# Graph convolution kernel: products of one-hot tiles and of sheet blocks in alternating order, and a third buffer for one-hot rows

## The chip, the cores and the metric

The kernel runs on one core of one Trainium2 chip. The metric is the device time of the whole program in microseconds (us), the median of several runs. A core has five engines with a queue each: TensorE (PE, whose weight loads are shown apart as PEld), VectorE (DVE), ScalarE (ACT), GpSimd (POOL) and SyncE (SP). They meet only at semaphores.

## The reference, cut to what matters

Two graph convolutions with normalisations between them, and then a mixture of eight feed-forward experts over the same 12500 nodes. The change touches the sum over edges, which each of the two convolutions has once:

```python
def _hconv(x, src, dst, ew, w1, b1, w2, b2, g, b):
    h = jax.nn.relu(x @ w1 + b1)
    msg = ew[:, None] * h[src]                                   # 200000 edges, 256 channels
    agg = jax.ops.segment_sum(msg, dst, num_segments=x.shape[0]) # edges are sorted by dst
    h = agg @ w2 + b2
    return jax.nn.relu(_bn(h, g, b))
```

The edges are sorted by dst, and dst is 12500 times the square of a uniform number: the low nodes have very many edges, the high ones few.

## The kernel before

The function `aggregate(layer)` runs once for each convolution. It sums the edges in two ways.

**Groups of gathers.** Edges are cut into tiles of 128, and four tiles (GT) make a group. For every tile, GpSimd issues one indirect DMA that fetches 128 rows of h from DRAM into one of R = 24 buffers `G` (`gather`, L982; the trace names the buffers wst, f_xr, f_u and more). VectorE makes a 128x128 one-hot matrix for each tile (`onehots`, L1180, 12 buffers `OH`). TensorE multiplies them, eight matmuls of 128x128 for a group (L1065, which the trace shows as 16 passes, since an fp32 matmul has two). VectorE adds the result into `agg` at the group's window (L1276). Before gathering the first tile of a group, GpSimd waits until TensorE has done the group that last used those buffers, six groups earlier (`g_mm`). Layer 0 has 291 such groups (1163 gathers), layer 1 has 271 (1083 gathers).

**Low groups.** Edges of the lowest nodes aren't gathered. They fall into "hot" tiles of 128 edges, 400 in layer 0 and 80 in layer 1. VectorE makes one-hot rows of the sources (`hot_rows`, L1189, into one of two buffers `HW`), ScalarE makes one-hot columns of the destinations (`lows`, L1113 and L1117, `LO`), TensorE multiplies them into `pX` (`hot_products`, L1019, two matmuls for a tile, four passes, two buffers), and VectorE adds the product to a count matrix `A` (`hot_add`, L1207). Such matrices are stored to DRAM as "sheets" by SP and loaded again in batches, and TensorE multiplies sheet blocks with rows of h (`unit`, L1033, two matmuls for a block, four passes, into `pF`). When a sheet is complete, VectorE adds it to `agg` (`seg_add`, L1223).

The two kinds of work are woven by a table that the program works out when it is built: `hot_behind(layer, q)` and `units_behind(layer, q)` list the hot tiles and the blocks that stand behind group q. In layer 0 there are one to three hot tiles behind each of the groups 0 to 193 (343 columns for a matmul shortly before group 80, 147 to 245 from there on), and none to three blocks behind the groups from 39 to 282. In layer 1 two hot tiles and one block stand behind each of the first 40 groups.

The order in time on each engine around this is:

- TensorE, for group q: wait for the one-hots and for the bank, eight matmuls of the group, then all hot tiles of the group, then all its blocks.
- VectorE, for group q: the one-hots of group q + 2, the add of group q (it waits for the group's matmuls), then for each hot tile t the rows of tile t + 1 and the add of tile t, then sheets that are complete.

The waits of a hot tile are these lines:

```python
g.wait_ge(hot_m, H0 + t + 1)          # TensorE: the rows of tile t are there
if t >= 2:
    g.wait_ge(hot_a, H0 + t - 1)      # TensorE: pX[t % 2] was added
...
if t >= 2:
    g.wait_ge(hot_p, H0 + t - 1)      # VectorE: HW[t % 2] was read
```

After the aggregation of a layer come its products with w2 (L1042, partly woven into the groups too), the normalisation, and, after layer 1, the experts.

Of the kernel before, what the change touches and what calls it, by code (L numbers as in the profile page):

```python
def build(nc, a, out):
# [5 lines left out]
    fp32, f32r, i32 = mybir.dt.float32, mybir.dt.float32r, mybir.dt.int32  # L7
# [3 lines left out]
    N, C = a["x"].shape  # L11
# [12 lines left out]
    NB = -(-N // P)  # L24
# [99 lines left out]
    A_W, WIN_W, LOW_W = NHG * HG * W_SEG, NB * W_WIN, GT * P  # L124
# [3 lines left out]
    with top:  # L128
# [22 lines left out]
        u = sb(top, "f_u", [P, KC, CH])  # L151
# [19 lines left out]
        ew_col = sb(edges, "ew_col", [P, GT * GW])  # L171
# [4 lines left out]
        key_col = sb(edges, "key_col", [P, GT * FG])  # L176
# [533 lines left out]
        NHOT = [GT * len(gs) for gs in HOT_G]  # L710
# [12 lines left out]
        def hot_behind(layer, q):  # L723
            return [t for t, at in enumerate(hot_q[layer]) if at == q]
# [24 lines left out]
        for layer in range(2):  # L749
            todo = [(p, b // HG, b) for p in range(len(USED[layer])) for b in range(NB)]  # L750
# [30 lines left out]
        def units_behind(layer, q):  # L781
            return [u for u, at in zip(units[layer], unit_at[layer]) if at == q]
# [4 lines left out]
        for layer in range(2):  # L787
            at = []
            for k in ADD_SEQ[layer]:
                i, j = SEG_AT[k]  # L790
# [47 lines left out]
        def aggregate(layer):  # L838
# [3 lines left out]
            with ExitStack() as s:  # L842
# [8 lines left out]

                upper = [agg[:, k, UPPER:AW] for k in range(KC)]
                A = [v[:, 0:A_W] for v in upper]
                HW = [v[:, A_W:A_W + WIN_W] for v in upper]
                steps = upper[0][:, A_W + WIN_W:A_W + 2 * WIN_W]
                LO = [upper[1][:, A_W + WIN_W + i * LOW_W:A_W + WIN_W + (i + 1) * LOW_W] for i in range(2)]

# [1 line left out]
                    AH = [sb(halves, f"ah{layer}_{i}", [P, KC, CH], f32r) for i in range(2)]  # L859
                early = [sb(s, f"early{layer}_{i}", [P, KC, CH]) for i in range(2)]  # L860
                AL = sb(s, f"al{layer}", [P, KC, CH], f32r)
                w2_raw = early[1][:, :, 0:C]
                window_row = early[0][0:1, 0, :].bitcast(i32)
                w2h, w2l = (sb(s, f"w2{layer}_{n}", [P, KC, C], f32r)[:, :, :] for n in ("hi", "lo"))
                work_w = max(2 * AB_W + 2 * HB_W, GT * GW + 2 * GW)
                work = sb(s, f"work{layer}", [P, work_w])
# [18 lines left out]
                t = f"x{layer}"  # L885
# [28 lines left out]
                with nc.Block() as block:  # L914
# [92 lines left out]
                    def _(g):  # L1007
                        def hot_products(t):

                            f, j, m, w, win = hot(layer, t)  # L1010
                            n = t // GT
                            g.wait_ge(hot_m, H0 + t + 1)
                            if j == 0:
                                g.wait_ge(hot_l, HG0 + n + 1)
                            if t >= 2:
                                g.wait_ge(hot_a, H0 + t - 1)
                            x = NB // 2 * win
                            for i in range(2):
                                ins = g.matmul(pX[t % 2][:, i * CH:i * CH + x], LO[n % 2][:, j * P:(j + 1) * P],  # L1019
                                               HW[t % 2][:, i * x:(i + 1) * x], start=True, stop=True)  # L1020
                            ins.then_inc(hot_p, 1)

                        def unit(p, hg, b):
# [31 lines left out]
                        for q in range(NQ):  # L1055
                            g.wait_ge(g_oh, E0 + q + 1)
                            if bank_of[q] in bank_of[0:q]:
                                g.wait_ge(g_add, E0 + max(x for x in range(q) if bank_of[x] == bank_of[q]) + 1)
                            elif q >= 2:
                                g.wait_ge(hot_a, H0 + NHOT[layer])  # L1060
                            for k in range(KC):
                                for t in tiles_of[q]:
                                    if k == 0:
                                        g.wait_ge(ga[t % R], gathered_value(layer, t))
                                    ins = g.matmul(pS[bank_of[q]][:, k, :], G[t % R][:, k * P:(k + 1) * P], OH[t % RO][:, :],  # L1065
                                                   start=t == tiles_of[q][0], stop=t == tiles_of[q][-1])
                            ins.then_inc(g_mm, 1)
                            for t in hot_behind(layer, q):
                                hot_products(t)
                            for u in units_behind(layer, q):  # L1070
                                unit(*u)
                            for n in chunks_behind(layer, q - 2):
                                product(n)
                        for n in chunks_after(layer, NQ - 2):
# [98 lines left out]
                    def _(g):  # L1173
# [9 lines left out]

                        def hot_rows(t):
                            f, j, m, w, win = hot(layer, t)
                            if t >= 2:
                                g.wait_ge(hot_p, H0 + t - 1)
                            c, e = j * FG + f, j * GW + f
                            g.tensor_scalar(HW[t % 2][:, 0:NB * win], steps[:, 0:NB * win], key_col[:, c:c + 1], ew_col[:, e:e + 1],  # L1189
                                            ALU.is_equal, ALU.mult).then_inc(hot_m, 1)  # L1190

                        def hot_add(t):
# [58 lines left out]
                            for name, some in (("base", regs), ("hot_at", hot_regs), ("seg_at", seg_regs)):  # L1251
                                some += [g.alloc_register(f"{name}{i}") for i in range(BATCH)]
                        g.wait_ge(steps_set, layer + 1)
                        hot_rows(0)
                        for q in range(AG):
                            onehots(q)
                        for q in range(NQ):
# [17 lines left out]
                                    g.wait_ge(agg_set, LOWER_SET)  # L1275
                            g.tensor_tensor(win, win, pS[bank_of[q]][:, :, 0:P], ALU.add).then_inc(g_add, 1)  # L1276
                            for t in hot_behind(layer, q):
                                if t + 1 < NHOT[layer]:
                                    hot_rows(t + 1)
                                hot_add(t)  # L1280
                            if adds_behind(layer, q):
                                g.wait_ge(g_add, E0 + q + 1)
# [807 lines left out]
```

## Time and profile before

| | |
|---|---|
| Median of 3 runs | 5071.51 us (5067.69 to 5071.55) |
| The profiled execution | 5075.8 us, of which the span in the trace is 5073.9 us |
| PE, DVE, POOL, ACT busy | 92%, 56%, 44%, 40% of the span |
| Gathers of layer 0 | about 165 to 1680 us of the span |
| Gathers of layer 1 | about 1823 to 3200 us |
| Experts | from about 3270 us to the end |

The busy share is a mean over these stages, which have different limits. In the rows below, idle time of an engine is put down to what released the instruction behind it; "issue" is time in which it waited for nothing that the profile shows. Names such as px or work are buffers with their numbers left out, and L1019 is line 1019 of the kernel before.

### The profile page before, as it was taken

The numbers are of one execution on the slowest core, as the hardware profiler recorded it, in microseconds if no ns is written. First come the engines' busy times: TensorE is split into PE (matmuls) and PEld (weight loads), VectorE is DVE, ScalarE is ACT, GpSimd is POOL, SyncE is SP. The second block draws the span as 40 slices with busy tenths as digits, with TensorE's granted clock in tenths as the row PEclk, the third lists the DMA queues.
The fourth block names the chain that finished last, engine by engine and source line by source line (L and its number), as shares of the span: only waits on it lengthen the run. The fifth ranks groups of instructions, "written<-read, shape, count | busy, mean of one in ns | idle before, by whom it ended". The sixth has DMA issues, their size and how long they took to land. (4 is left out here: it accounts for less than half of the span.)

```text
span 5073.9 us, 70560 instructions
## 1 busy us (share of the span) xinstructions
PE 4653.0 (92%) x25835; PEld 3759.1 (74%) x25835; DVE 2832.4 (56%) x6674; ACT 2036.5 (40%) x2999; POOL 2226.7 (44%) x2371
## 2 busy tenths in 40 slices
PE   7789988999999589999899998489999999999999
PEld 6667777777776577776666666378888888888888
DVE  7667666675443777433333333555666566655665
ACT  5533222332110543100000000467777777777777
POOL 1577776777777257777777777100000000000000
PEclk9889999999999799999999999689999999999999
DMA  5568765677655268877666665210000000000000
GB/s 166 165 187 266 235 193 186 210 231 240 213 203 200 66 210 258 270 237 242 219 237 234 223 236 165 81 50 17 22 26 26 18 22 26 26 24 19 22 21 11
DMA packets 507579, 722.88 MB, mean 142 GB/s; under 512 B 165259, under 2 KB 403150, under 8 KB 500833
## 3 DMA queue, kind: packets, MB, share of 16 engines
q1 hardware_dynamic: 390092, 407.69, 24.4%
q0 software_dynamic: 109360, 297.04, 18.8%
q10 hardware_dynamic: 7781, 13.60, 0.7%
q8 instruction: 209, 3.42, 0.3%
q14 instruction: 137, 1.12, 0.1%
HBM read 580.52 MB, written 137.63 MB: 142 GB/s over the span
## 5 line engine op out<-in xcount | busy, mean ns | idle before, releaser
L1033 PE MATMUL pf<-work 128*128 128x288 f32 (+3 forms) x2744 | 1040.0, 515 | 8.9 <-DMA work<-front 7.1
L1899 DVE TENSOR_TENSOR f_hl<-f_hf,f_hh 128x1024 fp32r<-128x1024 f32 (+1 forms) x400 | 479.6, 1199 | 707.6 <-ACT f_hf L1743 707.6
L982 POOL DMA_INDIRECT wst<-h,src_col x755 | 732.7, 970 | 235.9 <-issue 218.2
L982 POOL DMA_INDIRECT more<-h,src_col x744 | 719.3, 967 | 238.1 <-issue 216.2
L1736 ACT ACTIVATE f_hh<-f_p,f_sh,f_sc 128x512 fp32r<-128x512 f32 (+1 forms) x800 | 571.8, 768 | 438.2 <-PE f_p L2003 437.5
L1033 PEld LDWEIGHTS pf<-work 128*128 128x128 f32 x2744 | 499.6, 192 | 315.2 <-issue 263.3
L1148 ACT ACTIVATE ah<-agg 128x1024 fp32r<-128x1024 f32 (+1 forms) x50 | 51.8, 1037 | 1480.6 <-DVE agg L1276 1480.0
L1180 DVE TENSOR_SCALAR oh<-lane,rel_col,ew_col 128x128 f32<-128x128 f32 x2246 | 632.2, 360 | 0.0
L1276 DVE TENSOR_TENSOR agg<-agg,ps 128x256 f32 x398 | 167.4, 421 | 764.0 <-PE ps L1065 748.7
L1019 PE MATMUL px<-agg 128*128 128x343 f32 (+4 forms) x1920 | 517.3, 393 | 77.3 <-DVE agg L1189 74.1
L1743 ACT ACTIVATE f_hf<-f_p,f_sh,f_sc 128x512 f32<-128x512 f32 (+1 forms) x800 | 572.7, 776 | 0.0
L1019 PEld LDWEIGHTS px<-agg 128*128 128x128 f32 x1920 | 315.2, 194 | 208.4 <-DVE agg L1189 166.0
L982 POOL DMA_INDIRECT f_xr<-h,src_col x375 | 366.7, 978 | 119.4 <-issue 109.1
L982 POOL DMA_INDIRECT f_u<-h,src_col x372 | 360.8, 970 | 116.1 <-issue 109.4
L1113 ACT ACTIVATE agg<-lane,low_col 128x128 f32<-128x128 f32 x480 | 153.2, 390 | 587.1 <-PE px L1019 587.1
L1207 DVE TENSOR_TENSOR agg<-agg,px 128x686 f32 (+4 forms) x480 | 327.6, 682 | 97.5 <-PE px L1019 48.1
L1276 DVE TENSOR_TENSOR agg<-agg,px 128x256 f32 x164 | 69.0, 421 | 518.4 <-PE px L1065 518.4
L1065 PEld LDWEIGHTS ps<-oh,wst 128*128 128x128 f32 x2144 | 279.3, 202 | 97.0 <-DMA wst<-h,src_col 45.0
L1065 PE MATMUL ps<-oh,wst 128*128 128x128 f32 x2144 | 291.1, 289 | 57.3 <-DMA wst<-h,src_col 56.0
L1911 DVE SCALAR_TENSOR_TENSOR f_x<-f_p,f_gate,f_x 128x256 f32<-128x256 f32 x784 | 324.3, 475 | 2.4 <-PE f_p L2060 2.4
L2060 PE MATMUL f_p<-Wo_hi,f_hh 128*128 128x256 f32 (+1 forms) x1568 | 316.6, 283 | 1.9 <-DVE f_x L1911 1.9
L2060 PE MATMUL f_p<-Wo_lo,f_hh 128*128 128x256 f32 (+1 forms) x1568 | 315.8, 283 | 0.0
(265 smaller groups left out, 8030.7 us busy)
## 6 DMA issues: line engine op xcount, KB each, us to landing
work<-h SPq DMA_DIRECT2D x168, 512.0 KB
work<-front SPq DMA_DIRECT2D x50, 1024.0 KB
front<-agg SPq DMA_DIRECT2D x37, 1200.0 KB
work<-front SPq DMA_DIRECT2D x50, 816.0 KB
front<-agg SPq DMA_DIRECT2D x25, 1600.0 KB
work<-front SPq DMA_DIRECT2D x50, 576.0 KB
work<-front SPq DMA_DIRECT2D x25, 960.0 KB
a_x<-in_x SPq DMA_DIRECT2D x24, 512.0 KB, 4.5
```

What stands on the lines that cost most here:

```text
L982: g.indirect_dma_start(G[t % R], None, h_dram[layer], bass.IndirectOffsetOnAxis(ap=src_col[:, col:col + 1], axis=0)).then_inc(ga[t % R], 16)
L1019: ins = g.matmul(pX[t % 2][:, i * CH:i * CH + x], LO[n % 2][:, j * P:(j + 1) * P], HW[t % 2][:, i * x:(i + 1) * x], start=True, stop=True)
L1033: ins = g.matmul(pF[:, k, 0:count * w].rearrange("p (s c) -> p s c", c=w), HB[a % 2][0:r, n, k * P:(k + 1) * P], x, start=b == 0, stop=b = ...
L1065: ins = g.matmul(pS[bank_of[q]][:, k, :], G[t % R][:, k * P:(k + 1) * P], OH[t % RO][:, :], start=t == tiles_of[q][0], stop=t == tiles_of[ ...
L1180: ins = g.tensor_scalar(OH[t % RO][:, :], lane[:, :], rel_col[:, col:col + 1], ew_col[:, col:col + 1], ALU.is_equal, ALU.mult)
L1207: g.tensor_tensor(v, v, x.rearrange("p i (h c) -> p i h c", c=win), ALU.add).then_inc(hot_a, 1)
L1276: g.tensor_tensor(win, win, pS[bank_of[q]][:, :, 0:P], ALU.add).then_inc(g_add, 1)
L1736: ins = g.activation(hhi[l][q % 2][:, m, 0:nn], p[:, m, 0:nn], ACT.Relu, bias=shift[l][:, col], scale=scale[l][:, col])
L1743: ins = g.activation(hf[l][:, m, 0:nn], p[:, m, 0:nn], ACT.Relu, bias=shift[l][:, col], scale=scale[l][:, col])
L1899: g.tensor_tensor(hlo[l][q % 2][:, :, 0:nn], hf[l][:, :, 0:nn], hhi[l][q % 2][:, :, 0:nn].bitcast(fp32), ALU.subtract).then_inc(f_lo[l], 1)
L1911: ins = g.scalar_tensor_tensor(X1[0:r, j, :], p3[0:r, j, :], gate[c % 2][0:r, j, e:e + 1], X1[0:r, j, :], ALU.mult, ALU.add)
L2060: ins = g.matmul(p3[0:r, j, :], x[:, k, j * P:j * P + r], w[:, e, k, :], start=n == 0 and k == 0, stop=n == 2 and k == KC - 1)
```

## The change

Behind a group, TensorE no longer does all hot tiles and then all blocks, but a hot tile, a share of the blocks, the next hot tile, and so on. There is a third buffer for one-hot rows (`HW[2]`, in the buffer `early_0`, where a small row of window numbers lay, which moves to `early_1`), and VectorE makes the rows of tile t + 2, no longer t + 1, ahead of the add of tile t. Which tiles and blocks stand behind which group isn't changed, and no engine gets more matmuls, vector work or DMAs.

```diff
-                w2_raw = early[1][:, :, 0:C]
-                window_row = early[0][0:1, 0, :].bitcast(i32)
+                window_row = early[1][0:1, 1, :].bitcast(i32)
+                w2_raw = early[1][:, 0, :].rearrange("p (k n) -> p k n", n=C)
+                HW = [v[:, A_W:A_W + WIN_W] for v in upper] + [early[0][:, :, :].rearrange("p k n -> p (k n)")[:, 0:WIN_W]]
+                RH = len(HW)
...
                         def hot_products(t):
-                                               HW[t % 2][:, i * x:(i + 1) * x], start=True, stop=True)
+                                               HW[t % RH][:, i * x:(i + 1) * x], start=True, stop=True)
...
-                            for t in hot_behind(layer, q):
-                                hot_products(t)
-                            for u in units_behind(layer, q):
-                                unit(*u)
+                            hots, todo = hot_behind(layer, q), units_behind(layer, q)
+                            share = -(-len(todo) // max(len(hots), 1))
+                            for n in range(max(len(hots), 1)):
+                                if n < len(hots):
+                                    hot_products(hots[n])
+                                for u in todo[n * share:(n + 1) * share]:
+                                    unit(*u)
...
                         def hot_rows(t):
-                            if t >= 2:
-                                g.wait_ge(hot_p, H0 + t - 1)
+                            if t >= RH:
+                                g.wait_ge(hot_p, H0 + t - RH + 1)
...
-                        hot_rows(0)
+                        for t in range(RH - 1):
+                            hot_rows(t)
...
                             for t in hot_behind(layer, q):
-                                if t + 1 < NHOT[layer]:
-                                    hot_rows(t + 1)
+                                if t + RH - 1 < NHOT[layer]:
+                                    hot_rows(t + RH - 1)
                                 hot_add(t)
```

On TensorE, behind group 101 of layer 0, which has three hot tiles and two blocks (ps is the group's bank, px a hot tile's, pf the sheet's), this stands before:

```order
L1065 MATMUL ps_1<-oh_11,more 128x128
L1019 MATMUL px_0<-agg 128x147 x2
L1019 MATMUL px_1<-agg 128x147 x2
L1019 MATMUL px_0<-agg 128x147 x2
L1033 MATMUL pf<-work 128x288 x4
```

And this after, at the same place:

```order
L1066 MATMUL ps_1<-oh_11,more 128x128
L1020 MATMUL px_0<-early_0,agg 128x147 x2
L1034 MATMUL pf<-work 128x288 x2
L1020 MATMUL px_1<-agg 128x147 x2
L1034 MATMUL pf<-work 128x288 x2
L1020 MATMUL px_0<-agg 128x147 x2
```

One block has moved in behind the first hot tile and one behind the second; the eight matmuls of the group ahead of them stand as they were.

On VectorE, at the start of layer 0's groups, this stands before (the rows of a hot tile are L1189, the one-hots of gathered tiles L1180; the `ISA` rows read registers):

```order
L1189 TENSOR_SCALAR agg<-agg,key_col,ew_col 128x588
L1180 TENSOR_SCALAR oh_0<-lane,rel_col,ew_col 128x128
...
L1180 TENSOR_SCALAR oh_11<-lane,rel_col,ew_col 128x128
L1262 TENSOR_LOAD base_row
L1276 ISA
L1276 TENSOR_TENSOR agg<-agg,ps_0 128x2x128
L1189 TENSOR_SCALAR agg<-agg,key_col,ew_col 128x588
L1198 TENSOR_LOAD early_0
L1207 ISA
L1207 TENSOR_TENSOR agg<-agg,px_0 128x98x6
```

And this after:

```order
L1194 TENSOR_SCALAR agg<-agg,key_col,ew_col 128x588 x2
L1185 TENSOR_SCALAR oh_0<-lane,rel_col,ew_col 128x128
...
L1185 TENSOR_SCALAR oh_11<-lane,rel_col,ew_col 128x128
L1268 TENSOR_LOAD base_row
L1282 ISA
L1282 TENSOR_TENSOR agg<-agg,ps_0 128x2x128
L1194 TENSOR_SCALAR early_0<-agg,key_col,ew_col 128x588
L1203 TENSOR_LOAD early_1
L1212 ISA
L1212 TENSOR_TENSOR agg<-agg,px_0 128x98x6
```

The rows of two tiles are made at the start, and from there the order of kinds is the same: behind the add of a group come rows, add of a hot tile, rows, add; but each rows instruction is now for the tile after the next, and every third goes to early_0.

## Rows read from the trace of the kernel before

**Rows 1.** Stretches: busy PE, PEld, DVE, ACT, POOL (instructions); granted clock, DMA share, GB/s.

```profile
300.00:600.00 300.00, 271.87 (x1482) 213.43 (x1482) 209.67 (x470) 94.41 (x136) 229.30 (x233) 0.97 0.81 244
600.00:750.00 150.00, 134.30 (x869) 116.20 (x870) 95.96 (x280) 38.77 (x91) 114.04 (x119) 1.00 0.59 185
750.00:1250.00 500.00, 465.27 (x2691) 372.15 (x2690) 323.61 (x867) 141.66 (x252) 360.36 (x376) 0.99 0.70 219
1250.00:1500.00 250.00, 247.05 (x1271) 177.95 (x1270) 116.88 (x322) 32.57 (x33) 191.16 (x194) 1.00 0.61 208
...
1820.00:3200.00 1380.00, 1274.21 (x6486) 928.23 (x6486) 573.16 (x1643) 136.25 (x168) 1047.46 (x1084) 0.96 0.70 230
```

**Rows 2.** Waits of POOL, 750 to 1250: total us, times, longest.

```profile
POOL wst L982 <- issue: 33.2, 109, 0.3
...
POOL more L982 <- PE ps L1065: 18.0, 22, 2.9
...
POOL wst L982 <- PE ps L1065: 11.9, 19, 1.4
POOL f_xr L982 <- PE ps L1065: 7.9, 9, 2.9
POOL f_u L982 <- PE ps L1065: 5.5, 9, 1.1
```

**Rows 3.** Waits of POOL, 1820 to 3200 (layer 1), the largest on PE.

```profile
POOL wst L982 <- PE ps L1065: 3.0, 10, 0.3
```

**Rows 4.** Passes of L1065 on PE in two stretches.

```profile
600.00:750.00 150.00, 50.63 (x416) 1.00 0.59 185
750.00:1250.00 500.00, 185.71 (x1519) 0.99 0.70 219
```

**Rows 5.** Waits of PE, 600 to 750.

```profile
PE px L1019 <- DVE agg L1189: 16.0, 30, 1.0
```

**Rows 6.** Waits of PE, 750 to 1250.

```profile
PE px L1019 <- DVE agg L1189: 32.9, 85, 4.1
```

**Rows 7.** Timeline 702 to 706, PE and DVE: start us, us, what, [idle before].

```profile
702.04 0.67 PE L1019 MATMUL px<-agg 128*128 128x147 f32 x4
...
702.35 0.42 DVE L1276 TENSOR_TENSOR agg<-agg,ps 128x256 f32 x1 [1.22 <-PE ps L1065]
702.68 0.43 DVE L1189 TENSOR_SCALAR agg<-agg,key_col,ew_col 128x294 f32<-128x294 f32 x1
...
703.03 0.50 DVE L1207 TENSOR_TENSOR agg<-agg,px 128x294 f32 x1
...
703.17 1.52 PE L1019 MATMUL px<-agg 128*128 128x147 f32 x8 [0.46 <-DVE agg L1189]
703.43 0.43 DVE L1189 TENSOR_SCALAR agg<-agg,key_col,ew_col 128x294 f32<-128x294 f32 x1
...
704.52 1.13 PE L1033 MATMUL pf<-work 128*128 128x288 f32 x4
```

**Rows 8.** Timeline 789 to 797, around the add of a sheet.

```profile
789.46 3.05 DVE L1223 TENSOR_TENSOR agg<-agg,pf 128x64 f32 x9 [0.98 <-issue]
...
794.27 2.33 PE L1019 MATMUL px<-agg 128*128 128x147 f32 x8 [4.11 <-DVE agg L1189]
```

**Rows 9.** Waits of DVE, 750 to 1250.

```profile
DVE agg L1276 <- PE ps L1065: 135.9, 83, 6.9
DVE agg L1207 <- PE px L1019: 22.3, 80, 0.8
```

**Rows 10.** Groups of DVE instructions by shape: count, busy us, mean ns; 600 to 1250.

```profile
L1189 DVE TENSOR_SCALAR agg<-agg,key_col,ew_col 128x294 f32<-128x294 f32 x121 | 52.5, 434 | 0.0
...
L1189 DVE TENSOR_SCALAR agg<-agg,key_col,ew_col 128x490 f32<-128x490 f32 x72 | 39.3, 546 | 0.0
```

**Rows 11.** Timeline 1669 to 1673, DVE and POOL.

```profile
1669.81 1.23 DVE L1232 TENSOR_TENSOR al<-agg,ah 128x1024 fp32r<-128x1024 f32 x1
1670.22 1.63 POOL L982 DMA_INDIRECT wst<-h,src_col  x1 [0.31 <-issue]
```

More of the change, by code:

```diff
@@ L853, in aggregate @@
                 A = [v[:, 0:A_W] for v in upper]
-                HW = [v[:, A_W:A_W + WIN_W] for v in upper]
                 steps = upper[0][:, A_W + WIN_W:A_W + 2 * WIN_W]
@@ L1185, in hot_rows @@
                             f, j, m, w, win = hot(layer, t)
-                            if t >= 2:
-                                g.wait_ge(hot_p, H0 + t - 1)
+                            if t >= RH:
+                                g.wait_ge(hot_p, H0 + t - RH + 1)
                             c, e = j * FG + f, j * GW + f
-                            g.tensor_scalar(HW[t % 2][:, 0:NB * win], steps[:, 0:NB * win], key_col[:, c:c + 1], ew_col[:, e:e + 1],
+                            g.tensor_scalar(HW[t % RH][:, 0:NB * win], steps[:, 0:NB * win], key_col[:, c:c + 1], ew_col[:, e:e + 1],
                                             ALU.is_equal, ALU.mult).then_inc(hot_m, 1)
```

## Prediction

> **What bounds the kernel now.** I read the stretches first, then the waits of GpSimd, of TensorE and of VectorE. In the gather stages the clock of the kernel is GpSimd, which issues one gather after another. In the stretch from 750 to 1250 us a gather keeps it busy 360.36 / 376 = 0.958 us [rows 1], and 33.2 / 109 = 0.305 us pass before the next where nothing is waited for [rows 2]. That is 1.263 us for a gather and 5.05 us for a group of four. All later work of a layer stands behind its last gather, so GpSimd's pace sets the end of each layer unless GpSimd itself is held up.
>
> It is held up in one place. From 750 to 1250 us it waits for TensorE's group matmuls (L1065) 22 + 19 + 9 + 9 = 59 times, 18.0 + 11.9 + 7.9 + 5.5 = 43.3 us in total [rows 2]. Each of these contains the 0.305 us that pass anyway, 18.0 us together, so 25.3 us are lost. The stretch itself says the same: 500 - 360.36 - 376 x 0.305 = 25 us. In layer 1 such waits are 0.3 us each (3.0 us in 10), which is no loss [rows 3].
>
> Why does TensorE hold it up there? TensorE did 416 / 16 = 26.0 groups from 600 to 750 us and 1519 / 16 = 94.9 from 750 to 1250 [rows 4], while GpSimd issued 119 / 4 = 29.75 and 376 / 4 = 94 [rows 1]. So TensorE fell back by 3.75 groups, some 19 us, before GpSimd stood still (the ring holds six groups), and from there both move at TensorE's pace. That pace has two parts. TensorE's own work is 134.30 / 26.0 = 5.17 us a group in the first stretch and 465.27 / 94.9 = 4.90 in the second [rows 1, 4]. On top come waits for one-hot rows: 16.0 us [rows 5] and 32.9 us [rows 6], 0.62 and 0.35 us a group. They are all of TensorE's idle time there but 1.8 us. The timeline shows one: the first hot tile's products take 0.67 us; meanwhile VectorE, released by the same group's matmuls, does the add of the group and only then the next tile's rows, and TensorE stands 0.46 us [rows 7].
>
> **The change part by part.** *Rows two tiles ahead, third buffer.* Where rows of the second tile were made while the first was multiplied, they are now there before the group begins. The 0.46 us wait of [rows 7] goes wherever a group has two tiles. With three tiles, the third tile's rows are made right behind the group's add, 0.43 us of work [rows 7], while TensorE does the first. VectorE's instructions are the same ones. The extra rows instruction at the start of a layer (434 to 546 ns at the widths in [rows 10], somewhat more at that place, where it is wider) lies under the first gathers and costs nothing; without that cover it would be under 1 us a layer.
>
> *Blocks between tiles.* A block takes 1.13 us for its four passes [rows 7]. It gives VectorE that time for the rows and for the add that frees pX, so the other possible wait of a tile, on the add two tiles earlier, stays covered: rows, add of a tile and the group's add are 0.43 + 0.50 + 0.42 us [rows 7]. The price is that VectorE gets the last tile later, by the share of blocks ahead of it (1.13 us for one). VectorE has room: it is busy 323.61 / 94.9 = 3.41 us a group [rows 1, 4] and stands (135.9 + 22.3) / 94.9 = 1.67 us a group [rows 9]. Its one-hots are two groups ahead, so nobody waits on the later ones. Switching from tile to block costs nothing visible: L1033 follows L1019 with no idle time in [rows 7]; were it 0.1 us at each of some one and a half added switches, that would be 0.15 us a group.
>
> *What stays.* When a sheet is added, VectorE is taken for 3.05 us and TensorE stood 4.11 us behind it [rows 8]. With one more tile prepared, TensorE gets one tile (0.67 us) further, so I leave 3.4 us of it. It is one place in the stretch.
>
> **The sum.** If the waits go, TensorE needs 5.17 us a group where GpSimd brings one each 5.05, for about 30 groups: it falls back 3 to 4 us more. After that it needs 4.90, and gains 0.15 us a group, 14 us over 95 groups. The 19 us from which GpSimd stands still aren't reached, with the 3.4 us of the sheet's add neither. So the whole 25.3 us go, at GpSimd's end of layer 0, and everything behind shifts. It needs only part of the waits to go: with w us of them left per group, the fall back by the end of the stretch is 29.75 x (0.12 + w) + 94.9 x (w - 0.15), which reaches 19 at w = 0.24. Now w is 48.9 / 120.9 = 0.40. Beyond 0.24 each 0.01 us costs 1.25 us.
>
> Nothing more is to be had: before 600 and after 1250 us, and in layer 1, GpSimd doesn't wait, so TensorE's waits there cost nothing. What could be less is the pace of the gathers once they run freely. From 300 to 600 us, unhindered, a gather takes 229.30 / 233 = 0.984 us, from 1250 to 1500 0.985, from 600 to 750, before the first loss, 114.04 / 119 = 0.958 [rows 1]. With 0.984 over 376 gathers the gain is 9.8 us less, 15.5 us. I take the value of the stretch itself, since the vector work that runs beside those gathers is that stretch's. Bounds of the gain: 15 and 28 us (the upper one with 0.5% of noise in the other gathers' 1.26 us turned into gain, 3 us over some 500).
>
> The sum stands against the profiled execution: 5075.8 - 25.3 = 5050.5 us. That run is 4.3 us above the median of the timed ones, 5071.51, so against the median it is **5046.2 us**.
>
> **Of the clock.** With TensorE busy 93% and 99% of a stretch (750 to 1250, 1250 to 1500) the granted clock is 0.99 and 1.00; with 91 and 92% (300 to 600, layer 1), where it keeps up with the gathers, 0.97 and 0.96, which is 2.4 GHz with short falls to 1.2; with 90% from 600 to 750 it is 1.00 all the same [rows 1], and no wait there is longer than 1.0 us [rows 5]. After the change TensorE works 4.90 / 5.05 = 97% of the long stretch and waits for gathers in the rest. The Trainium skill (TensorE: Matmul & The Clock Gate, section HAM oscillation) says that waits for DMAs between bursts of matmuls make the clock fall. The trace agrees in direction with its 0.96 and 0.97. By that rule the time could come out another way, as below.
>
> **Rivals.**
> 1. *The wait changes its name.* TensorE waits for the add of pX or for late rows behind the block, as VectorE now ends its round later. For it: VectorE already waits 22.3 us for products [rows 9], so the two run close to each other. Against: 1.67 us a group of room. If w falls only to 0.32, the loss is 1.25 x 8 = 10 us, the gain 15, the time 5056. Chance 0.13.
> 2. *The clock takes it.* If TensorE in 750 to 1250 us worked at 0.90, 4.90 would be 5.4 us a group, 0.39 us over GpSimd's pace, 37 us, of which 19 fit into the ring: 18 us of stalls, a gain of 7, 5064. Against: layer 1 at 0.96 holds GpSimd up by nothing [rows 1, 3]. Chance 0.04.
> 3. *Slower: gathers get longer.* GpSimd's gather becomes longer when certain VectorE work meets it: 1.63 us where a subtraction of two SBUF tiles of 1.23 us ran [rows 11], against 0.958. If the new order made such meetings more frequent, each 0.030 us on the mean of the 840 or so gathers of layer 0 from 600 us on costs 25 us and eats the gain; that is the point from which it decides. At 0.045 us the kernel is 12 us slower, 5084. Against: the rows and one-hots are the same instructions, the long subtraction isn't moved, and in 600 to 1250 us, full of rows, the mean is 0.958. Chance 0.04. The Trainium skill (SBUF — State Buffer, on DMAs issued by GpSimd) says that VectorE's two-port instructions lock GpSimd out while it writes descriptors. The rows instruction gains 196 columns for 112 ns [rows 10], 0.57 ns each. By the rule every meeting would block for up to the instruction's length; the 0.958 us mean doesn't show it.
> 4. *No effect.* What holds TensorE back isn't the waits but its total work, which stretches as the waits go: 5071. Against: its work alone is 4.90 us a group, under GpSimd's 5.05, and the waits are nearly all the rest [rows 1, 6]. Chance 0.05.
>
> **How the numbers follow.** The forecast, a gain of 20 to 28 us, has 0.74. With 5046 as its time, the range goes from 5041 (its upper bound of gain with the runs' own spread of 2 us) to 5058, which takes in rival 1 and slower gathers and leaves out rivals 2 to 4 (0.13) and the forecast's tails. What a measurement of this kernel can tell from no change is 0.2%, 10 us. Faster by more: the forecast and rival 1, 0.87. Within: rivals 2 and 4, 0.09. Slower: rival 3, 0.04.
>
> **What would show it.** Right: in layer 0 GpSimd's waits on L1066 (the line L1065 has now) become 0.3 us each, the last gather of layer 0 is issued some 25 us earlier, TensorE's waits for rows (L1194) nearly vanish between 600 and 1250 us and give way to short waits for gathers, and layer 1 and the experts take as long as before. Wrong: waits of L1020 on L1212 (the add), a mean gather above 0.97 us in that stretch, a clock under 0.96 there, or a layer 1 that changes its length.

## The result, and the profile after

| | before | changed kernel |
|---|---|---|
| Median | 5069.6 us (5063.75 to 5071.55, 4 runs) | 5038.44 us (5034.66 to 5040.63, 4 runs) |
| Profiled execution | 5075.8 us, span 5073.9 | 5039.27 us, span 5037.4 |

The ratio is 0.9939 (0.9924 to 0.9954), 31 us less (23 to 38). The median is 2.6 us below the range. The interval of this comparison by itself would still allow the 25.3 us of the sum; together with four comparisons below (the changed kernel again, its parts, a shorter ring) the gain is 27.3 to 31.2 us, 2 to 6 us more than the sum. The four runs of before include the three that the prediction stood on, whose median was 2 us higher.

Stretches of the changed kernel, columns as in [rows 1]:

```profile
300.00:600.00 300.00, 271.56 (x1503) 222.15 (x1503) 207.44 (x475) 95.79 (x141) 229.02 (x234) 0.95 0.81 243
600.00:750.00 150.00, 140.36 (x959) 127.87 (x959) 105.53 (x305) 41.48 (x97) 114.06 (x119) 0.99 0.64 203
750.00:1250.00 500.00, 469.31 (x2774) 392.16 (x2773) 331.94 (x894) 142.80 (x247) 379.74 (x395) 0.98 0.73 228
1250.00:1500.00 250.00, 245.52 (x1229) 173.06 (x1227) 110.50 (x299) 29.52 (x30) 190.79 (x195) 1.00 0.60 203
```

From 750 to 1250 us there are now 395 gathers, where there were 376 [rows 1]: 19 x 1.263 = 24 us of gathering more in the same time. A gather takes 379.74 / 395 = 0.961 us. The granted clock is 0.99 and 0.98, 2.4 GHz nearly throughout.

Waits of GpSimd in the same stretch (total us, times, longest), against [rows 2]; L983 and L1066 are L982 and L1065 of before:

```profile
POOL wst L983 <- issue: 41.1, 135, 0.3
POOL more L983 <- issue: 39.9, 131, 0.3
POOL f_u L983 <- issue: 19.5, 64, 0.3
POOL f_xr L983 <- issue: 18.9, 62, 0.3
POOL f_xr L983 <- PE ps L1066: 0.6, 2, 0.3
POOL wst L983 <- PE ps L1066: 0.3, 1, 0.3
```

59 waits on TensorE have become 3, each of the 0.3 us that pass before any gather. Nothing is lost there any more. Passes of L1066 on TensorE, as in [rows 4]:

```profile
600.00:750.00 150.00, 60.35 (x466) 0.99 0.64 203
750.00:1250.00 500.00, 206.32 (x1600) 0.98 0.73 228
```

That is 466 / 16 = 29.1 groups in the first stretch (before 26.0) and 100 in the second (before 94.9). GpSimd brings 29.75 in the first, so TensorE nearly keeps up. Its waits, from 600 to 750 us and then from 750 to 1250, against [rows 5, 6]:

```profile
PE ps L1066 <- DMA more<-h,src_col: 4.4, 7, 1.3
PE ps L1066 <- DMA wst<-h,src_col: 4.2, 3, 2.1
...
PE px L1020 <- DVE agg L1212: 0.2, 1, 0.2
...
PE ps L1066 <- DMA more<-h,src_col: 7.4, 9, 2.2
PE px L1020 <- DVE agg L1212: 5.9, 5, 4.5
PE ps L1066 <- DMA f_u<-h,src_col: 4.7, 7, 1.0
```

There is no wait for rows (L1194) left. What TensorE waits for is gathers, the sign that it now keeps up with GpSimd, and the add (L1212), 5.9 us in 5 waits of which one is 4.5. The timeline of one group with two hot tiles shows the new order (rows of PE and DVE alone: start us, us, what, [idle before]):

```profile
691.93 0.67 PE L1020 MATMUL px<-agg 128*128 128x147 f32 x4
692.23 0.42 DVE L1282 TENSOR_TENSOR agg<-agg,ps 128x256 f32 x1
692.43 1.13 PE L1034 MATMUL pf<-work 128*128 128x288 f32 x4
692.57 0.43 DVE L1194 TENSOR_SCALAR early<-agg,key_col,ew_col 128x294 f32<-128x294 f32 x1
692.91 0.45 DVE L1212 TENSOR_TENSOR agg<-agg,px 128x294 f32 x1
693.28 0.43 DVE L1194 TENSOR_SCALAR agg<-agg,key_col,ew_col 128x294 f32<-128x294 f32 x1
693.40 0.67 PE L1020 MATMUL px<-agg 128*128 128x147 f32 x4
693.91 1.13 PE L1034 MATMUL pf<-work 128*128 128x288 f32 x4
```

VectorE does the group's add, rows and the add of the first tile under that tile and the block behind it. The second tile starts without the 0.46 us of [rows 7].

Where the 36.5 us between the two spans lie, read from the first and last gather of each layer. One line of the changed kernel for each layer (count, shortest/median/longest ns, first to last start; the gather that ends the layer is among them):

```profile
L983 POOL DMA_INDIRECT f_xr<-h,src_col x195: 942/946/1963, 178.3 to 1651.2; - x195
...
L983 POOL DMA_INDIRECT wst<-h,src_col x363: 942/946/1956, 1794.8 to 3166.3; - x182
```

| us | before | after | difference |
|---|---|---|---|
| to the first gather | 167.1 | 168.1 | -1.0 |
| gathers of layer 0, first to last start | 1511.3 | 1483.2 | 28.1 |
| from there to the first gather of layer 1 | 145.1 | 143.5 | 1.5 |
| gathers of layer 1 | 1375.5 | 1371.5 | 4.0 |
| from the last gather to the end | 1874.9 | 1871.1 | 3.8 |

Of the 28.1 us, 25.4 are GpSimd's lost waits over all of layer 0: in before it waited for TensorE 81 times, 49.9 us in total, and 49.9 - 81 x 0.303 = 25.4; in the changed kernel 22 times, 6.7 us, with nothing lost. The other rows are of the size by which two executions of one kernel differ, as the first experiment shows.

How far TensorE is behind can be counted from the same traces: gathers started, divided by four, less passes of L1065 (L1066) started, divided by sixteen. The ring holds six groups.

| groups behind, at us | 600 | 700 | 750 | 800 | 1250 |
|---|---|---|---|---|---|
| before | 2.0 | 4.8 | 5.5 | 5.3 | 4.3 |
| changed kernel | 1.9 | 1.8 | 2.4 | 2.5 | 1.0 |

In before the first wait of over 0.4 us comes at 759 us. Counted every 5 us over layer 0, the changed kernel's TensorE is never more than 2.6 groups behind, so the ring doesn't fill.

### The profile page after: what moved, and what is told of

Its sections match the earlier page's. It is cut to its first block and busy times, and to the rows that moved or that the text cites. A ratio compares the mean times of both kernels' runs of the same rounds, so it can differ in the third digit from the quotient of the medians.

```text
span 5037.4 us, 70560 instructions
## 1 busy us (share of the span) xinstructions
PE 4617.2 (92%) x25835; PEld 3773.7 (75%) x25835; DVE 2828.7 (56%) x6674; ACT 2034.9 (40%) x2999; POOL 2221.1 (44%) x2371
## 5 line engine op out<-in xcount | busy, mean ns | idle before, releaser
L1034 PE MATMUL pf<-work 128*128 128x288 f32 (+3 forms) x2744 | 1050.6, 518 | 7.6 <-DMA work<-front 6.5
L983 POOL DMA_INDIRECT wst<-h,src_col x755 | 730.5, 968 | 229.8 <-issue 225.5
L983 POOL DMA_INDIRECT more<-h,src_col x744 | 719.0, 966 | 226.6 <-issue 223.9
L1212 DVE TENSOR_TENSOR agg<-agg,px 128x686 f32 (+4 forms) x480 | 327.6, 682 | 172.6 <-PE px L1020 142.3
L983 POOL DMA_INDIRECT f_xr<-h,src_col x375 | 364.0, 971 | 114.3 <-issue 111.2
L983 POOL DMA_INDIRECT f_u<-h,src_col x372 | 360.5, 969 | 113.3 <-issue 111.5
L1066 PE MATMUL ps<-oh,wst 128*128 128x128 f32 x2144 | 290.2, 286 | 75.5 <-DMA wst<-h,src_col 75.2
L1066 PEld LDWEIGHTS ps<-oh,wst 128*128 128x128 f32 x2144 | 273.9, 198 | 112.4 <-DMA wst<-h,src_col 63.0
L1020 PE MATMUL px<-agg 128*128 128x343 f32 (+4 forms) x1284 | 331.6, 384 | 7.0 <-DVE agg L1212 6.9
L1066 PEld LDWEIGHTS ps<-oh,more 128*128 128x128 f32 x2112 | 266.2, 195 | 83.9 <-DMA more<-h,src_col 55.8
L1066 PE MATMUL ps<-oh,more 128*128 128x128 f32 x2112 | 280.8, 283 | 46.3 <-DMA more<-h,src_col 45.6
```

The lines of the kernel that those rows point to most:

```text
L983: g.indirect_dma_start(G[t % R], None, h_dram[layer], bass.IndirectOffsetOnAxis(ap=src_col[:, col:col + 1], axis=0)).then_inc(ga[t % R], 16)
L1034: ins = g.matmul(pF[:, k, 0:count * w].rearrange("p (s c) -> p s c", c=w), HB[a % 2][0:r, n, k * P:(k + 1) * P], x, start=b == 0, stop=b = ...
L1212: g.tensor_tensor(v, v, x.rearrange("p i (h c) -> p i h c", c=win), ALU.add).then_inc(hot_a, 1)
```

## The experiments

The kernels ran on four chips, each with runs of before beside them. The first and the third chip show the known times. On the second and the fourth all kernels take about 9% longer. A ratio is always to before on the same chip. "Lost in layer 0" is GpSimd's idle time before gathers of layer 0 that waited for TensorE, less 0.303 us for each. Edits are to the changed kernel, except for `before_ring20`.

**Both kernels once more.** No edit: `before_again` is the kernel before, `after_again` the changed one.

> The kernel before once more, for a second profile of it. Theory A: 1372 to 1376 us from first to last gather in layer 1 and a tail behind it of 1871 to 1875 us, so that both differ between profiles of one kernel as much as between the two kernels. Theory B: 1375 us in layer 1 again. Both: GpSimd loses 25 to 27 us to waits for TensorE in layer 0.

> The changed kernel once more. Theory A (all of the gain is GpSimd's 25.8 us of lost waits in layer 0; what the first comparison showed beyond it is scatter between executions): a ratio near 0.9950, a gain of 24 to 28 us, and the gathers' pace in layer 1 not the same as in the first profile, 1371 to 1376 us from first to last gather. Theory B (the change also shortens gathers and layer 1 by some 6 us, as VectorE's work meets them less): a ratio of 0.9938 or less, a gain of 31 us or more, and 1371 to 1372 us for layer 1 again.

Before: one run, 5066.17 us, span 5064.3, 9.6 us less than in the execution that the sum was made against. Changed: 5039.93 us (5038.35 to 5047.44) against 5067.49 us (9 runs), ratio 0.9949 (0.9936 to 0.9963). Layer 0 takes 1509.5 and 1480.5 us, 29.0 less; 25.6 and 0.0 us are lost. Layer 1 takes 1373.6 and 1374.2, from its last gather to the end 1871.8 and 1872.3: no gain in either. So the 4.0 and 3.8 us of the table above aren't shown to be the change's by these two pairs (for layer 1, more below).

**Each part alone.** `alt_only` has the new order on TensorE and the two row buffers of before, `rows_only` the third buffer and the order of before.

```diff
 alt_only
-                RH = len(HW)
+                RH = 2
 rows_only
-                            for n in range(max(len(hots), 1)):
-                                if n < len(hots):
-                                    hot_products(hots[n])
-                                for u in todo[n * share:(n + 1) * share]:
-                                    unit(*u)
+                            for t in hot_behind(layer, q):
+                                hot_products(t)
+                            for u in units_behind(layer, q):
+                                unit(*u)
```

> Alternating order alone, rows one tile ahead in two buffers as before. With a block (1.1 us) behind the first tile, the 0.46 us wait for the second tile's rows is covered; in groups with no block, or with a third tile and one block, a wait stays. Theory A with my threshold (0.24 us of waits a group left): waits fall from 0.40 to about 0.1 us a group, nothing is lost by GpSimd, the time is that of the full change within 2 us, 5039 to 5044. Rival (the third buffer does the work): waits stay above 0.24 us, GpSimd loses 10 us or more, 5050 or more.

> Third buffer and rows two tiles ahead alone, all tiles of a group and then all blocks as before. The second tile's rows are there; the third tile, or the second's successor, waits for the add that frees its product buffer (0.43 + 0.50 + 0.42 us of VectorE work against 1.3 us of two tiles), a few tenths in groups of three. Theory A: 0.1 to 0.2 us a group left, under the threshold, GpSimd loses nothing or a few us, 5039 to 5047. Rival (alternation does the work): GpSimd loses 10 us or more, 5050 or more.

`alt_only`: 5040.14 us (5037.21 to 5042.37), ratio 0.9948 (0.9934 to 0.9961). `rows_only`: 5036.78 us (5035.1 to 5038.34), ratio 0.994 (0.9926 to 0.9953). Either part alone gives all of it: the intervals of the two ratios overlap with each other and with that of the changed kernel, and `rows_only` is even 2 us under what was expected of it. Lost in layer 0: under 0.1 us in both. TensorE's waits for VectorE, first `alt_only` and then `rows_only`, for 600 to 750 and 750 to 1250 us:

```profile
PE px L1020 <- DVE agg L1194: 0.6, 2, 0.5
...
PE px L1020 <- DVE agg L1194: 7.3, 10, 4.1
```

```profile
PE px L1020 <- DVE agg L1209: 11.6, 20, 1.3
...
PE px L1020 <- DVE agg L1209: 12.1, 20, 4.4
```

With the block between, even rows made one tile ahead come in time: 7.9 us of waits where there were 48.9. With the third buffer and tiles in a row, the waits for rows are gone, but 23.7 us for the add (L1209 there) have come: the wait changes its name and shrinks by half. It costs nothing all the same: it is 0.18 us a group, under the 0.24 from which the prediction saw a loss, and TensorE is at most 3.6 groups behind in layer 0, where the ring holds six.

**Between the two: alternation in every fourth group.** Two row buffers, and the new order only where q is a multiple of four.

```diff
-                RH = len(HW)
+                RH = 2
-                            share = -(-len(todo) // max(len(hots), 1))
-                            for n in range(max(len(hots), 1)):
-                                if n < len(hots):
-                                    hot_products(hots[n])
+                            parts = max(len(hots), 1) if q % 4 == 0 else 1
+                            share = -(-len(todo) // parts)
+                            for n in range(parts):
+                                for t in hots[n:n + 1] if parts > 1 else hots:
+                                    hot_products(t)
```

> Rows one tile ahead, and the alternating order in every fourth group alone; the other groups keep the old order. By the prediction's formula (threshold at 0.24 us of waits a group, 1.25 us of loss for each 0.01 us beyond) the waits stay at 0.32 us a group, GpSimd loses 10 us, gain 15, about 5053. By the corrected account from the traces of the changed kernel (TensorE takes 5.77 us a group from 600 to 750 us before and 4.82 of its own work after, 5.27 and 4.69 from 750 to 1250; 19 us fit into the ring), a quarter of the difference taken off leaves 30 x 0.48 + 95 x 0.075 = 21.6 us of fall back, a loss of 3 us, gain 23, about 5044.

> The alternating order in every fourth group alone, once more, since in the first comparison every kernel, the one before too, took some 450 us longer and GpSimd stood at every second group in all of them. If the kernel before is at 5067 us again: 10 us lost by GpSimd in layer 0 and 5053 by the prediction's formula, 3 us lost and 5044 by the account corrected from the traces.

On the second chip it took 5513.79 us, ratio 0.9991 (0.9982 to 1.0). On the third, with the known times, 5051.09 us (5050.1 to 5051.94) against 5069.49 us (15 runs), ratio 0.9961 (0.9948 to 0.9975). Waits there, in the two stretches, and what GpSimd's idle time before gathers of layer 0 ended with (us, times):

```profile
PE px L1020 <- DVE agg L1195: 11.4, 23, 1.0
...
PE px L1020 <- DVE agg L1195: 26.1, 65, 4.1
...
  issue: 341.7, 1122
  PE ps L1066: 15.2, 34
  PE px L1066: 2.1, 7
```

The waits for rows are 37.5 us over 28.0 + 98.0 groups, so w, the waits for each group in the prediction's sum, is 0.30. Lost in layer 0: 15.2 + 2.1 - 41 x 0.303 = 4.9 us, between the 10 and the 3 us that the two accounts in the expectation gave. TensorE is 4.0 groups behind at 750 us and 5.0 at 800, so the ring fills later than in before. The rule of the prediction, 1.25 us for each 0.01 above 0.24, gives 7 for this w, and 20 for the 0.40 of before, where 25 are lost. So a w of 0.40 loses 25, 0.30 loses 5, 0.18 and less nothing. There is a threshold, and it lies between 0.18 and 0.30; these runs don't place it closer. That the time, 18 us under before, is near the 5053 of the first account is in part luck: another 4.2 us are lost in layer 1, in three waits from 2049 to 2071 us, which neither account had.

**The ring one group shorter.** `before_ring20` and `after_ring20` are the two kernels with twenty gather buffers instead of 24, five groups.

```diff
-        R, RO = 24, 12
+        R, RO = 20, 12
```

> The kernel before with 20 buffers for gathered rows, five groups and not six. Theory A (what GpSimd loses is TensorE's fall back beyond what the ring holds): it loses one group's time more, 25.8 + 5 = 31 us, in layer 0, and 0 to 2 us in layer 1, 5 to 7 us slower than before. Rival (GpSimd waits because of the landing time of gathers or something else than the fall back): the loss doesn't move by a group's time, but stays at 26 us or doubles.

> The changed kernel with 20 buffers. Theory A: TensorE doesn't fall back at all there, so a ring of five groups is as good as one of six: GpSimd loses 0 to 1 us in layer 0 and the time is that of the changed kernel within 2 us. Rival (the change has only just brought the fall back under the ring's size): GpSimd loses 3 to 5 us.

> The kernel before with a ring of five groups, once more for the same reason. Theory A: one group's time more lost, 31 us in layer 0, and up to 2 us in layer 1; 5 to 7 us slower than before. Rival, from the first comparison, where it was 11 us faster than before: it is faster here too, and the tail behind the last gather is some 6 us shorter.

> The changed kernel with a ring of five groups, once more. Theory A: as the changed kernel within 2 us, GpSimd loses 0 to 1 us in layer 0. Rival, from the first comparison, where its gain was 42 us: some 10 us faster than the changed kernel here too.

On the second chip: before with 20 buffers 5505.95 us, ratio 0.998 (0.9971 to 0.9989); changed 5475.07 us, ratio 0.9921 (0.9908 to 0.9935). On the third: before with 20 buffers 5081.33 us (5076.96 to 5084.72), ratio 1.0021 (1.0012 to 1.003); changed 5039.31 us, ratio 0.9938 (0.9924 to 0.9951). GpSimd's idle time before gathers of layer 0 in before with 20 buffers, third chip:

```profile
  issue: 328.6, 1079
  PE ps L1065: 55.3, 79
  PE px L1065: 1.5, 5
```

Lost: 55.3 + 1.5 - 84 x 0.303 = 31.3 us against 25.4 and 25.6, 5.8 more, about one group's time of 5.05. That shows what the ring does by itself: TensorE falls behind as before, and the ring takes in one group less of it. Another 3.2 us are lost in layer 1, where 0 to 2 were expected, and the whole is 12 us slower than before by the medians (6 to 15 by the ratio), where 5 to 7 were expected. The changed kernel loses nothing with five groups, as with six: TensorE doesn't fall behind far enough to use the ring. A ring of more than six groups wasn't tried.

Layer 1 is nearer to such a loss than its waits of 0.3 us tell. Counted as in the table above, TensorE is 5.0 groups behind at 2083 us in before; with the order and rows of before in layer 1 it loses 0.0, 0.3 and, with five groups, 3.2 us there, and 4.2 with the order of before in three groups of four. In the changed kernel it is at most 3.1 groups behind in that layer (3.5 in its second profile) and loses nothing.

**One layer alone.** Order and third buffer as changed in one layer, as before in the other (of `layer1_only` read 1 for 0 and 0 for 1).

```diff
-                RH = len(HW)
+                RH = len(HW) if layer == 0 else 2
...
-                            share = -(-len(todo) // max(len(hots), 1))
+                            share = -(-len(todo) // max(len(hots), 1)) if layer == 0 else 0
...
+                            if layer == 1:
+                                for u in todo:
+                                    unit(*u)
```

> Both parts of the change in layer 0 alone; layer 1 has its old order and its rows one tile ahead. Theory A (the gain is GpSimd's lost waits in layer 0): the whole gain, within 2 us of the changed kernel, 5037 to 5042, and 1370 to 1376 us from first to last gather in layer 1. Theory B (layer 1 gains 3 to 4 us from the change as well): 3 to 4 us slower than the changed kernel, 5042 or more, and 1374 to 1376 us in layer 1.

> The change in layer 0 alone, once more, beside the kernel before with its usual time. Theory A: 25 to 28 us faster than before, as the whole change, and 1370 to 1376 us in layer 1. Theory B: 3 to 5 us of the gain missing, and 1373 to 1376 us in layer 1.

> The change in layer 1 alone; layer 0 has its old order and its rows one tile ahead. Theory A (layer 1 gains nothing, as GpSimd never waits there; what was measured beyond 25.8 us is scatter): the time of before within 2 us, 1370 to 1376 us from first to last gather in layer 1. Theory B (TensorE's and VectorE's new order makes layer 1's gathers faster): 3 to 5 us faster than before, and 1368 to 1372 us in layer 1.

Both chips were of the slower kind. Layer 0 alone: 5488.65 us against 5517.51 (20 runs), ratio 0.9949 (0.9936 to 0.9963), and on the fourth chip 5486.22 against 5519.2 (15 runs), again 0.9949 (0.9936 to 0.9963). Layer 1 alone: 5509.71 us, ratio 0.9989 (0.998 to 0.9998). So 29 and 33 us by the medians come from layer 0 (28 by the ratio), and 9 from the other edit (6 by the ratio, 1 to 11), of which layer 1's gathers account for 6: they take 1577.9, 1579.4, 1580.1 and 1579.2 us in four profiles with layer 1 as before, and 1573.6, 1573.0 and 1572.2 in three with it changed. This holds for chips on which GpSimd is held up in layer 1 too (last section). With the known times the same comparison is 1375.5 and 1373.6 against 1371.5, 1374.2, 1370.8, 1367.9 and 1372.3: means 3.2 us apart, the two sets overlapping. So neither theory of the expectations holds as it stands: layer 1 does gain on the slower chips, and on the others it isn't resolved.

**Both kernels on a chip of the slower kind**, one run of each.

> A third profile of the kernel before, for the scatter between executions. Theory A: from first to last gather in layer 1 between 1370 and 1376 us, so that the ranges of both kernels overlap. Theory B: 1373 to 1376 us, above all profiles of the changed kernel but one.

> A third profile of the changed kernel, for the scatter between executions. Theory A: 1370 to 1376 us in layer 1. Theory B: 1368 to 1372 us. Both: GpSimd loses under 1 us in layer 0 and the gathers of layer 0 take 1480 to 1484 us.

Before 5516.78 us, changed 5479.81 us, 37.0 less: layer 0 1732.4 to 1702.1 us, layer 1 1577.9 to 1573.6. The expectations of 1370 to 1376 and 1480 to 1484 us were for the known times and aren't met on this chip.

**A version that uses the room.** TensorE now has about 4.8 us of work for a group where GpSimd brings one every 5.05. `sheet21` gives it more of the low groups, so that fewer edges are gathered: four groups less in each layer.

```diff
-              (24, [(17, 1, 7)]),
+              (24, [(21, 1, 7)]),
```

> The changed kernel with four more low groups: the third sheet has 21 segments, not 17, so each layer gathers four groups less and layer 0 has 16 hot tiles more, and the blocks of that sheet are 504 columns wide, not 408. Theory A says that the gathers' pace alone bounds both stages and that TensorE has 0.2 to 0.3 us a group of room after the change: 8 groups less at 5.05 us, less what the added TensorE work (98 blocks by about 0.35 us, 16 tiles by 1.3 us, in layer 0; 98 blocks in layer 1) takes beyond that room: 30 to 40 us faster than the changed kernel, about 5003. Rival (TensorE is the bound right after the change): no gain, 5035 or more.

4998.19 us (4995.53 to 5000.65), ratio 0.9855 (0.984 to 0.987): 71 us under before on the same chip, 41 under the changed kernel with twenty buffers there (5039.31). Eight groups of 5.05 us are 40.4. Layer 0 has 1147 gathers and takes 1459.0 us, layer 1 1067 and 1357.0. Its stretches:

```profile
600.00:750.00 150.00, 144.97 (x964) 130.10 (x963) 110.99 (x313) 45.74 (x98) 113.77 (x119) 0.98 0.69 219
750.00:1250.00 500.00, 487.20 (x2781) 386.05 (x2780) 333.57 (x890) 148.81 (x262) 379.96 (x395) 0.99 0.74 235
```

GpSimd still issues 395 gathers from 750 to 1250 us and loses 0.2 us in the layer. But TensorE is busy 97% of that stretch, and behind it, at 1500 us, it is 5.4 groups behind (1.4 in the changed kernel): the ring is all but full, and a further step would begin to lose there. None was tried.

## Why the prediction was right, and where it fell short

**The bound and the loss: right.** GpSimd's 25.4 us of lost waits went to nothing, and layer 0 became shorter by that and a little. Waits on TensorE of 0.3 us, no more waits for rows, waits for gathers in their place: each line that was to show it is there. Of the signs of the wrong case two came: L1020 waiting on L1212, which costs nothing, and a layer 1 that changes its length, shown on the slower chips.

**The fall back: right, and shown; its threshold right in kind.** The changed kernel, the two parts alone, every fourth group, before and the shorter ring fit one account (w 0.05 to 0.40, losses 0 to 25, and 5.8 us for one group of ring). The sum behind it doesn't close, though: with w = 0.40 it gives a fall back of 39 us, 20 beyond the ring's 19, where the prediction itself reads 25.3 lost. The number 0.24 isn't confirmed, only that the threshold lies between 0.18 and 0.30.

**TensorE's own work: mis-sized.** The prediction had 5.17 and 4.90 us a group. With the waits gone it is 140.36 / 29.1 = 4.82 and 469.31 / 100 = 4.69. A part of this is that the changed kernel gets to other groups in the same stretch. Over the same groups the busy time is 5.12 and 4.88 (groups 83 to 109) and 4.94 and 4.78 (110 to 189). `rows_only`, with the order of before, has 4.85 and 4.74, so it isn't the order. The busy time of before held part of the waits, it seems: weight loads showed longer waits for the same rows than matmuls did, in this line of before from 600 to 750 us, against the 16.0 us of [rows 5]:

```profile
PEld px L1019 <- DVE agg L1189: 25.6, 46, 1.2
```

So waits that go take some busy time with them, which the formula for w leaves out. From 600 to 750 us, where the sum had TensorE at its limit and falling back 3 to 4 us, it now waits 9.3 us for gathers.

**The sheet's add: mis-sized, without effect.** 4.5 us of it stay, not 3.4 (4.6 in the second profile): the third tile's product now waits for the add behind the sheet instead of for its rows. The ring takes it in.

```profile
768.49 3.06 DVE L1228 TENSOR_TENSOR agg<-agg,pf 128x64 f32 x9 [0.95 <-issue]
...
773.81 1.32 PE L1020 MATMUL px<-agg 128*128 128x147 f32 x4 [4.51 <-DVE agg L1212]
```

**"Nothing more is to be had": the step that failed.** The prediction took the gathers' pace as something that could cost 9.8 us or give 3 at most, and put layer 1's gain at nothing. It gave more. Layer 0 takes 1510.4 us on the mean in two profiles of before and 1482.4 in five with the new order, the new rows or both: 28.0 us less, of which 25.5 are lost waits and 2.5 the pace. Layer 1 may have given 3.2 us more, which the times don't resolve.

The traces show where it comes from. In before none of the 719 gathers with no VectorE instruction beside their first 0.9 us took longer than 0.959 us; beside rows (L1189) 78 of 505 took more than 1.1 us, beside one-hots (L1180) 3 of 834. Such long gathers number 65 and 65 in layer 0 in two profiles of before and 57, 48, 36, 58 and 58 in the five others, and in layer 1 40 and 37 against 29, 35, 28, 32 and 24. What all gathers take beyond 0.946 us each falls from 31.7 to 29.6 us in layer 0 and from 21.2 to 18.1 in layer 1, on the mean. So fewer gathers are lengthened beside VectorE's work once the order behind a group moves. Why just these are wasn't tried, and 2 to 3 us a layer are near the scatter between two executions: the single values overlap.

**The median stood on: off by 2 to 4 us.** The three runs had 5071.51. All runs of before on chips with the known times have medians of 5067.5 to 5069.6. From 5069.6 the forecast would have been 5044.3. Taken against before on the same chip, the gain is 31.2 us, 27.6 (both kernels once more), 27.3 and 30.7 (the parts alone) and 30.2 (with the short ring), about 29 where 25.3 were forecast and 28 was the upper bound. Both errors go the same way. From 5069.6 the lower end of the range would have been 5039.6, still 1 us above the time.

**The rivals.** *The wait changes its name*: it did, and fully so in `rows_only`, but at 0.18 us a group and less it costs nothing. *The clock*: 0.99 and 0.98 in the long stretches. The Trainium skill (TensorE: Matmul & The Clock Gate, section HAM oscillation) has waits for DMAs between bursts of matmuls make the clock fall. Here TensorE waits for gathers from 600 to 1250 us, 2.4 us at the longest, and the clock goes from 1.00 and 0.99 to 0.99 and 0.98 (in `alt_only` to 0.97 and 0.98): the trace agrees in direction, but the fall is small. *Gathers longer*: 0.961 us against 0.958 [rows 1]. The Trainium skill (SBUF — State Buffer, the "DVE blocks DMA" trap) would have them blocked by VectorE's two-port work; with more VectorE instructions in these 500 us than before (894 for 867) the mean moved by 0.003 us. The means hide that the rule shows in some: the 78 of 505 above. *No effect*: fell at once.

## What to carry to other kernels

Find the engine that issues the stage's work and count what it loses; the consumer's waits are worth that much, however many there are. Then draw up an account of three things: the producer's pace, the consumer's work plus its waits, and what the ring between them holds. It tells how much waiting the consumer can afford before a loss begins, and that two edits which each bring the waits under that mark are worth the same as both. Check how full the ring gets, not only whether the producer waits: a stage without a loss can be close to one. The busy time of a pipelined engine can contain some of its waits, as here, so room shows larger once they are gone, and that room may be worth more than the change itself (41 us here, by moving work from the producer to the consumer).

## What the runs showed of the hardware

Two of the four chips take 5517.5 and 5519.2 us for a kernel that takes 5067 to 5070 on the others. Of the 451 us between two profiles of before 427 lie in the gather stages, layer 0 1732.4 us for 1509.5, layer 1 1577.9 for 1373.6, with a gather itself as long as ever (median 0.946 us); 12 lie behind the last gather. GpSimd stands there at the first gather of about every second group:

```profile
2606.52 0.95 POOL L982 DMA_INDIRECT f_u<-h,src_col  x1 [0.30 <-issue]
2610.13 0.94 POOL L982 DMA_INDIRECT more<-h,src_col  x1 [2.66 <-remote]
...
2627.47 0.94 POOL L982 DMA_INDIRECT wst<-h,src_col  x1 [2.61 <-remote]
...
2645.17 0.94 POOL L982 DMA_INDIRECT more<-h,src_col  x1 [2.61 <-remote]
```

From a group's last gather to its last pass on TensorE it is 30 us there in before and 27 in the changed kernel (medians in layer 0), against 15 and 8 on the other chips, and from the third or fourth group on. The packets aren't what is late: they take as long (median 159 ns), and counted every 5 us from 250 to 1600 us, the bytes moved are no further behind the gathers issued than on the other chips (0.3 of a gather less on the mean), while TensorE is about five groups behind instead of two in the changed kernel. With five groups in the ring it isn't slower there (ratio 0.998). What is late between the packets and TensorE isn't settled: the ring isn't what bounds it, and the profile names the releaser mostly as "remote". The whole change gives 37 us there, in one run of each kernel.
